# Attention on one core: score and maximum products in four pieces of 32 stationary columns, value products as they were

## What is computed

```python
def self_attention(x):                  # 2048 queries, 2048 keys
    q, k, v = split(x @ w_qkv)          # 16 heads of 16
    q, k = layernorm(q), layernorm(k)
    att = softmax(q @ k.T / 4, axis=-1)
    return (att @ v) @ w_proj
def cross_attention(x, y):              # 2048 queries, 1601 keys
    q, k, v = x @ Wq + bq, *split(y @ Wkv + bkv)
    return (softmax(q @ k.T / 4) @ v) @ Wo + bo
x = x + self_attention(layernorm(x))
x = x + cross_attention(layernorm(x), ctx)
...
```

## Time and profile before

| | us |
|---|---|
| median of 3 executions | 1681.9 |
| lowest, highest | 1680.58, 1682.75 |
| span of the profiled execution | 1681.4 |
| PE busy in the span | 1598.4 (95%) |
| DVE busy in the span | 1499.6 (89%) |
| ACT busy in the span | 1319.1 (78%) |

### The profile page before, as it was taken

The page is one execution under the profiler, slowest core; times in us unless marked ns, Lnnn a source line. Parts: engine busy times, 40 slices in busy tenths (PEclk is TensorE's granted clock), DMA queues, the critical chain, the costliest instruction groups (busy, mean ns, idle before and its releaser), DMA issues. The chain is left out here.

```text
span 1681.4 us, 36595 instructions
## 1 busy us (share of the span) xinstructions
PE 1598.4 (95%) x14449; PEld 634.1 (38%) x14452; DVE 1499.6 (89%) x2182; ACT 1319.1 (78%) x2590; POOL 406.3 (24%) x666
## 2 busy tenths in 40 slices
PE   6999999999999999999999999999989999889997
PEld 3542222222223232223322222222235555657774
DVE  6899999989999999989899999999948887688876
ACT  4618999879988989898899999999985565545544
POOL 5800110212223312312211111111013443533302
PEclk9999999999999999999999999999999999999999
DMA  4001001001101200101221011010002000015551
GB/s 147 14 7 20 14 14 14 14 14 22 31 14 21 45 14 14 33 17 27 70 55 26 14 21 20 14 27 14 14 28 63 1 1 1 1 31 95 101 102 51
DMA packets 148026, 52.32 MB, mean 31 GB/s; under 512 B 137424, under 2 KB 146128, under 8 KB 147600
## 3 DMA queue, kind: packets, MB, share of 16 engines
q1 hardware_dynamic: 147152, 48.62, 14.1%
q10 hardware_dynamic: 704, 1.38, 0.2%
HBM read 14.07 MB, written 2.10 MB: 10 GB/s over the span
## 5 line engine op out<-in xcount | busy, mean ns | idle before, releaser
L968 DVE TENSOR_REDUCE mxp<-ps_m 128x2 f32<-128x1024 f32 (+2 forms) x928 | 1049.3, 1198 | 41.3 <-PE ps_m L747 39.9
L897 ACT ACTIVATE work<-ps_s 128x512 f32<-128x512 f32 x1856 | 1001.7, 598 | 76.7 <-PE ps_s L771 48.9
L797 PE MATMUL ps_av<-work,vst 128*32 128x256 f32 x7424 | 592.8, 391 | 14.7 <-ACT avs L904 12.3
L771 PE MATMUL ps_s<-qb,k_stack 50*128 50x512 f16 x1856 | 565.8, 382 | 0.5 <-ACT v_rows L915 0.3
L747 PE MATMUL ps_m<-k_stack,qa 48*128 48x512 f16 (+1 forms) x2048 | 534.1, 358 | 2.3 <-PEq L1123 0.5
L797 PEld LDWEIGHTS ps_av<-work,vst 128*32 128x32 f32 x7424 | 147.0, 108 | 383.2 <-ACT work L897 321.6
L771 PEld LDWEIGHTS ps_s<-qb,k_stack 50*128 50x128 f16 x1856 | 119.7, 94 | 378.6 <-ACT work L897 323.4
L747 PEld LDWEIGHTS ps_m<-k_stack,qa 48*128 48x128 f16 x2048 | 108.2, 93 | 21.5 <-DVE mxp L968 14.8
L616 POOL TENSOR_SCALAR mtmp<-negm 128x16 f32<-128x16 f32 x32 | 8.2, 255 | 390.5 <-DVE negm L973 390.4
L602 POOL COPY vst<-v_rows 128x1024 f32<-128x1024 f32 (+1 forms) x32 | 30.6, 956 | 144.5 <-PE ps_av L797 144.5
L682 POOL TENSOR_TENSOR q_rows<-avs,rc 128x256 f32<-128x256 f32 x31 | 19.2, 619 | 173.3 <-DVE rc L979 173.3
(11 more groups left out here) (441 smaller groups left out, 2006.1 us busy)
## 6 DMA issues: line engine op xcount, KB each, us to landing
x_res<-in_x SPq DMA_DIRECT2D x4, 512.0 KB, 8.2
w_experts<-in_w_experts SPq DMA_DIRECT2D x1, 2048.0 KB, 8.0
out<-x_res SPq DMA_DIRECT2D x8, 256.0 KB, 2.2
v_rows<-in_ctx_c SPq DMA_DIRECT2D x1, 1664.0 KB, 7.3
work<-in_ctx_t SPq DMA_DIRECT2D x1, 1456.0 KB, 15.8
ctx_n<-in_ctx_n SPq DMA_DIRECT2D x1, 1248.0 KB, 8.0
w_qkv<-in_w_qkv ACTq DMA_DIRECT2D x1, 768.0 KB, 8.6
w_qkv<-in_w_qkv SPq DMA_DIRECT2D x1, 768.0 KB, 4.2
```

The lines of the kernel that those rows point to most:

```text
L771: pe.matmul(ps_s[:, bank, :], STACKS[part(n)][rows, group(n) * PAIRS + j, t * P:t * P + P], qb[n % 2][rows, :, j, :], start=True, stop=Tru ...
L797: m = pe.matmul(ps_av[32 * h:32 * h + 32, cols], vst[n % 2][:, t, h, :], pbuf[(tau[n] + t) % 2][:, h, cols], start=(t == 0 and half == 0), ...
L897: a.activation(pbuf[g % 2][:, h, :], ps_s[:, b, :], ACT.Exp, scale=factor).then_inc(s["exp"], 1)
L968: v.tensor_reduce(dst, src, AX.X, ALU.max).then_inc(s["mred"], 1)
```

## The change

`max_side` and `score_side` issue each product as four. The four read the same moving operand; each has 32 of the 128 stationary columns and writes the 32 partitions of the result that belong to them. On the array they are tiles of 64 rows by 32 columns. The semaphore is raised by the last of the four only (the last of the last piece for maxima). The waits, the banks, the order of units and everything on the other engines stay. The value products, transposes and projections are not touched. 1856 score products become 7424 and 2048 maximum products become 8192, with as many weight loads: 11712 more of each.

```diff
+QUARTER = [slice(c, c + 32) for c in range(0, P, 32)]
...
             def max_side(n, u, b, e):
-                g = part(n)
+                g, rows = part(n), slice(e * HALF, e * HALF + MAXROWS)
                 for a, j, key, width, col in pieces(g, u):
-                    m = pe.matmul(ps_m[:, b, e, col:col + width], qa[n % 3][e * HALF:e * HALF + MAXROWS, a, j, :],
-                                  STACKS[g][e * HALF:e * HALF + MAXROWS, group(n) * PAIRS + j, key:key + width],
-                                  start=True, stop=True)
+                    for q in QUARTER:
+                        m = pe.matmul(ps_m[q, b, e, col:col + width], qa[n % 3][rows, a, j, q],
+                                      STACKS[g][rows, group(n) * PAIRS + j, key:key + width], start=True, stop=True)
...
-                pe.matmul(ps_s[:, bank, :], STACKS[part(n)][rows, group(n) * PAIRS + j, t * P:t * P + P], qb[n % 2][rows, :, j, :],
-                          start=True, stop=True).then_inc(s["sc"], 1)
+                for q in QUARTER:
+                    m = pe.matmul(ps_s[q, bank, :], STACKS[part(n)][rows, group(n) * PAIRS + j, t * P + q.start:t * P + q.stop],
+                                  qb[n % 2][rows, :, j, :], start=True, stop=True)
+                m.then_inc(s["sc"], 1)
```

## The result

| us | before | after |
|---|---|---|
| median | 1681.24 (4 executions) | 1698.03 (4 executions) |
| lowest, highest | 1680.45, 1682.75 | 1695.61, 1699.99 |
| profiled execution, time | not recorded | 1695.61 |
| its span | 1681.4 | 1693.8 |

The ratio is 1.0098, with a 95% interval of 1.0085 to 1.0110: 16.8 us more. The forecast was 50 us more; its direction is right, its size is three times too large, and the time lies within the range of 1676 to 1800.

What follows compares the result with a forecast made beforehand. TensorE was taken to pace most halves at 1.108 us, VectorE 2% behind. Adding 0.060 per half gave 41.5 + 7.6 + 0.7, together 49.8 us on 1681.9: 1732 us, own range 1701 to 1757, 8-in-10 range 1676 to 1800.

Steps and rivals of the forecast that it cites:

- the two gaps: TensorE idle before and after the value products, 0.094 and 0.097 us, where tiling changes; both stay, 0 saved.
- A: Idle time around the value products vanishes or halves with equal columns, VectorE paces at 1.131; 1650 us; chance 0.11.
- C: Narrower loads shrink the idle time behind the values to about 0.03 us; time unchanged, 1680 us; chance 0.06.
- the stagger: First wave of a half: eight starts replace two, 7 ns apart, so the last starts at 0.046 us.
- the load delay: Second wave of a half: four loads of the next wave delay the running product by 0.027 us.
- low end: Cheapest case for TensorE's half: f16 starts 3 ns apart, +0.027 us per half, whole kernel 1701 us.
- the 205 halves that VectorE paces: Halves set by VectorE's 1.131 us, passed by TensorE's 1.168: 0.037 us more each, 7.6 us.
- the short pieces: Cross attention's small products, streaming 29 ns each; four column groups at 7 ns make 28, so no extra cost.
- the chunks' starts: 31 halves at a chunk's first key tile: values wait for ScalarE's copy, 0.37 us idle, covering the added 0.060.
- Projection halves: Halves containing projections: same two waves as the others, so 0.060 us more each, within the 692 halves' 41.5 us.
- Rival B: TensorE's instructions are not supplied fast enough; 2350 us at 0.082 us a pair, some 1940 at 62 ns; chance 0.08.
- Rival D: Narrow f16 loads come slower, say 14 ns apart: +0.139 us per half, 1800 us; chance 0.13 with other higher costs.

Runs made afterwards that it cites:

- the short reduce: Kernels before and after the change, each with VectorE reducing only 256 of every 512 maxima; 1658.48 us (before) and 1678.80 us (after).

## Why the prediction was right and wrong

**Right: the two gaps stay.** They are 0.308 and 0.309 after the change, and were 0.308 and 0.312 before it. The transposes of the earlier trace rows had shown that one changing dimension is enough, and the runs with values over 64 keys showed it for either. Rivals A and C fall with that. A's mechanism does come once the values use 64 rows: TensorE's half loses its gaps and VectorE paces. A's 1650 did not come even there: that kernel, which leaves out half of each sum, took 1681.86.

**Wrong in size: the stagger and the load delay, +0.060 a half.** The sum took 7 ns between starts from the f32 loads of the values and named 3 ns as its low end. The trace shows 3.3 ns for loads of f16, and 6.5 to 7 for f32 (the values over 64 keys have it too, on tiles of the same shape as the scores). Type, not shape, was the row to go by, and the 3 ns between a score and a maximum, both f16, were already there. So the first wave's last start came at 0.024, not at 0.046. The second term, 0.027 for the loads, came from the same f32 rows: the second wave begins 0.226 after the first, 0.011 over the 0.215 of a product, and it did so before the change too. The 0.060 was some 0.043 of stagger and some 0.016 of loads more than before; measured are 0.020 and 0, less the 0.003 behind the values, 0.018 in all. The low end of 0.027 lay above that as well. 505 intervals at 0.018 make 9 us; the sum had 41.5 for 692 at 0.060, and the others of those 692 add 4 us together.

**Wrong: what VectorE adds.** With TensorE at 1.126, below VectorE's 1.131, the 205 halves that VectorE paces cost nothing (+0.3 us in all; 7.6 in the sum), and its waiting rose by some 9 us, to 48.4 and not to 80 to 100.

**Wrong: the short pieces cost no more.** The sum compared streaming times: four column groups 7 ns apart for 29 ns of columns. It did not ask how many products stand between the first score and the last piece. Thirteen halves have 56 of them, more than the 32 pairs that TensorE takes ahead of the oldest product's end, and pay 0.232 each, 3.0 us (the half behind each gets 0.038 back). The earlier trace rows has only six, and could not show it.

**Nearly right: the chunks' starts.** The copy that the values wait for covers 19 of 30; 11 grow by 22 ns, probably because ScalarE's copy stands behind exponentials whose scores come later; that was not tested. It is 0.3 us in all. Projection halves grew by 40, not 60; 18 of it is the plain half's, the other 22 ns (0.7 us in all) go with VectorE's pace: with the short reduce these halves grow by 18, too.

**Rival B.** Something like its mechanism shows in the kernels with more products, at a pair per 29 to 30 ns over a long stretch and 8 to 9 ns in a short one, so a half with 24 pairs, one per 47 ns, does not meet it. The 62 ns per product of the Trainium skill, page "TensorE: Matmul & The Clock Gate", section "Wait — 56ns, not 53.3ns?", are not what these traces show, and the estimate from them falls: the kernel after does a plain half's 24 products in 1.126. (Both times given for B were summed too low: by the prediction's own halves, 692 and 205 of them, 1.97 us makes some 2450 and not 2350, and 1.49 some 2020 and not 1940.) **Rival D** is refuted by the 3.3 ns. The start of the last product at 0.250, below the 0.27 to 0.32 that I named, was the sign.

No kernel here that computes everything beats the one before. A version whose values are 64 by 32 tiles with both halves of the keys computed would need their sums brought together in further PSUM banks, and all eight are in use; it was not tried. My estimate is that it could gain no more than VectorE's waiting, 38.9 us, and the fall of the clock in the two kernels with 64 rows could take that back.

## What to carry to other kernels

Narrow tiles do not pay for themselves while another shape stands in the same loop: a switch in rows or in columns alone costs its full gap, and mixed shapes do not even share the array. Take the price of a start, and of the loads beside a running product, from a row of the same type as the new instruction: f32 rows gave twice the price of f16 here. And where a change multiplies small products, count how many stand between two long ones: the price came where 32 pairs were exceeded, and the next limit seems to be the long-run rate of instructions.

## What was not expected of the hardware

- Loads of f16 tiles start 3.3 ns apart at 32 and 64 columns; f32 tiles of 32 columns 6.5 to 7 ns, with 64 rows or 128.
- The second wave of products comes later than 0.215 us after the first, as I read it by the loads beside the running wave: by some 25 ns with four of 64 columns, by some 11 with eight of 32 or two of 128.
- Tiles of different shape wait for each other even on different rows: 0.32 us from start to start for products of 512 columns.
- At most 32 pairs of load and product are taken; the 33rd starts 0.413 after the first where that is 387 ns long, 0.306 where it is 280. Behind it a pair comes mostly every 8 to 9 ns.
- With one pair asked for every 26 ns all along, TensorE stood still 146 times for some 0.64 us, each time until 1.2 to 1.7 us after a 16.4 KB packet of instructions had landed.
- With value products over half the rows, the granted clock fell to its 1.2 GHz level for a part of two stretches of the block (0.71 and 0.60 in the mean from 1200 to 1260 us), where it stays at 1.00 with all rows.
